# Linear attention's feature passes: the squares of the projections move from VectorE to ScalarE

## The reference, cut to what matters

```python
def softmax_kernel_features(data, proj, is_query):
    d = data.shape[-1]                                   # 16
    data_normalizer = 1.0 / math.sqrt(math.sqrt(d))      # 0.5
    ratio = 1.0 / math.sqrt(proj.shape[0])
    data_dash = jnp.einsum('bhnd,md->bhnm', data_normalizer * data, proj)
    diag_data = jnp.sum(jnp.square(data), axis=-1, keepdims=True) * 0.5 * data_normalizer * data_normalizer
    stab = jnp.max(data_dash, axis=-1, keepdims=True) if is_query else jnp.max(data_dash)
    return ratio * (jnp.exp(data_dash - diag_data - stab) + EPS)
q1 = softmax_kernel_features(q, proj_mat, is_query=True)
k1 = softmax_kernel_features(k, proj_mat, is_query=False)
kv = jnp.einsum('bhnm,bhnd->bhmd', k1, v)
z = 1.0 / jnp.einsum('bhnm,bhm->bhn', q1, jnp.sum(k1, axis=2))
out = jnp.einsum('bhnm,bhmd->bhnd', q1, kv) * z[..., None]
```

## Time and profile before

| | us |
|---|---|
| median of three runs | 2383.1 |
| lowest and highest | 2375.92, 2383.48 |
| span of the profiled execution | 2403.1 |
| TensorE busy | 1879.3 (78%) |
| VectorE busy | 1495.5 (62%) |
| ScalarE busy | 1074.7 (45%) |
| GpSimd busy | 395.9 (16%) |

### The profile page before, as it was taken

The page is one execution under the profiler, slowest core; times in us unless marked ns, Lnnn a source line. Parts: engine busy times, 40 slices in busy tenths (PEclk is TensorE's granted clock), DMA queues, the critical chain, the costliest instruction groups (busy, mean ns, idle before and its releaser), DMA issues. The chain is left out here.

```text
span 2403.1 us, 30974 instructions
## 1 busy us (share of the span) xinstructions
PE 1879.3 (78%) x9780; PEld 1007.5 (42%) x9804; DVE 1495.5 (62%) x2518; ACT 1074.7 (45%) x1896; POOL 395.9 (16%) x595
## 2 busy tenths in 40 slices
PE   3868788858876453777668877998899984999994
PEld 2745655535333320000022234442133333888883
DVE  4558449966010687999878876999788883111114
ACT  1100222214110476999979964342477661222220
POOL 5000000000112010222100003331033343222221
PEclk8989999968887575555589978997799996999997
DMA  3011110005797004443011008777666703566664
GB/s 85 1 39 31 48 31 27 20 10 229 309 411 314 20 0 127 127 127 123 18 32 40 26 16 119 130 132 107 83 88 95 97 28 135 195 201 203 202 203 184
DMA packets 147792, 264.98 MB, mean 110 GB/s; under 512 B 28864, under 2 KB 115985, under 8 KB 142678
## 3 DMA queue, kind: packets, MB, share of 16 engines
q1 hardware_dynamic: 135750, 242.10, 38.0%
q0 software_dynamic: 10768, 18.19, 2.3%
q10 hardware_dynamic: 1152, 3.15, 0.3%
HBM read 221.85 MB, written 57.71 MB: 116 GB/s over the span
## 5 line engine op out<-in xcount | busy, mean ns | idle before, releaser
L1743 PE MATMUL ps<-arena 128*128 x376 | 194.9, 621 | 108.2 <-ACT ps L1785 60.1
L1785 ACT ACTIVATE ps<-ps,arena 128x512 f32<-128x512 f32 x384 | 256.7, 1121 | 6.3 <-POOL arena L1769 6.3
L1753 DVE TENSOR_REDUCE arena<-ps 128x1024 f32 x192 | 232.8, 1225 | 24.5 <-PE ps L1743 12.2
L1785 ACT ACTIVATION_READ_ACCUMULATOR ps<-ps,arena 128x1 f32 x384 | 234.7, 668 | 0.0
L2159 DVE TENSOR_REDUCE arena<-ps 128x1024 f32 x192 | 221.3, 1219 | 12.4 <-PE ps L2405 9.8
L2618 ACT ACTIVATE arena<-ps 128x1024 f32<-128x1024 f32 x192 | 185.1, 1020 | 97.6 <-PE ps L2500 96.4
L2962 DVE TENSOR_TENSOR arena<-ps,arena 128x384 f32<-128x384 f32 x39 | 21.8, 558 | 286.4 <-PE ps L2918 286.4
L2942 ACT ACTIVATE arena<-ps,arena 128x256 f32<-128x256 f32 x234 | 89.5, 481 | 235.9 <-PE ps L2907 230.0
L2405 PE MATMUL ps<-arena 96*128 96x512 bf16 x500 | 162.7, 430 | 26.4 <-DVE arena L2159 12.2
L1950 ACT ACTIVATE arena<-ps 128x1024 f32<-128x1024 f32 x192 | 178.7, 1048 | 7.8 <-DVE arena L1970 4.6
L529 PE MATMUL ps<-arena 96*128 96x456 f32 (+1 forms) x512 | 170.3, 482 | 8.8 <-DMA arena<-la_xt 5.2
(11 more groups left out here) (394 smaller groups left out, 3264.8 us busy)
## 6 DMA issues: line engine op xcount, KB each, us to landing
arena<-in_sm_w_dram SPq DMA_DIRECT2D x128, 576.0 KB, 15.5
arena<-in_re_w_dram SPq DMA_DIRECT2D x39, 1252.0 KB, 5.9
arena<-ra_parts SPq DMA_DIRECT2D x192, 192.0 KB, 9.1
routed_in<-routed_in SPq DMA_DIRECT2D x8, 3332.0 KB, 14.2
ra_parts<-arena SPq DMA_DIRECT2D x48, 192.0 KB, 2.4
arena<-routed_in SPq DMA_DIRECT2D x39, 196.0 KB, 5.4
arena<-la_xt SPq DMA_DIRECT2D x16, 384.0 KB, 3.4
arena<-arena SPq DMA_DIRECT2D x64, 96.0 KB, 2.2
```

The costliest lines, as they stand in the source:

```text
L1743: ins = pe.matmul(ps[:, 2 * (n % 4) + t % 2, :], QM[j][:, h, t * P:(t + 1) * P], KI[:, b, h // HG, :], start=True, stop=True)
L1753: v.tensor_reduce(MXq[:, b, 2 * u:2 * u + 2, at_head(h)], ps[:, 2 * (n % 4):2 * (n % 4) + 2, :], AX.X, ALU.max).then_inc(s_lk, 1)
L1785: ins = act.activation(bank, bank, ACT.Exp, bias=nb[n % 4][:, t % 2:t % 2 + 1], scale=c_reg, accum_out=RS[:, b, t, at_head(h):at_head(h) + 1])
```

## The change

ScalarE computes the squares straight from PSUM with one activation per tile, in both passes, and VectorE's copy and multiply go. The signals `ks` and `qs` say that the squares are there; VectorE's chain waits for them and no longer for the products. In the key pass ScalarE's program becomes squares 0 and 1, the copy of the next batch's turned rows, squares 2 and 3. In the query pass it becomes, for t from 0 to 4: square t+1 (for t = 4 that of tile 0 of the next batch; none for t = 3), Exp t, copy of turn t-1. The row maximum moves ahead of the sum of squares in both passes, in the query pass with a semaphore of its own (`s_mq`).

```diff
+    def squares(act, b, t, ready, done):
+        ready.wait(act, b, t + 1)
+        act.activation(SQ[t % 2], ps[:, 2 * (t % 2), 0:D], ACT.Square).then_inc(done.sem, 1)
     def squared_lengths(v, link, t):
-        q = ps[:, 2 * (t % 2), 0:D]
-        link(v.tensor_copy(SQ[t % 2], q))
-        link(v.tensor_tensor(SQ[t % 2], SQ[t % 2], q, ALU.mult))
         link(v.tensor_reduce(dg[t % 2], SQ[t % 2].rearrange("p (h d) -> p h d", h=NH), AX.X, ALU.add))
...
+    ks = S1("k_squares", T, 1)
...
                 for t in range(T):
-                    kp.wait(v, b, t + 1)
+                    ks.wait(v, b, t + 1)
+                    v.tensor_reduce(MX[:, bass.ds(b, 1), t], features(t), AX.XYZ, ALU.max)
                     squared_lengths(v, link, t)
-                    v.tensor_reduce(MX[:, bass.ds(b, 1), t], features(t), AX.XYZ, ALU.max)
...
+            def square(b, t):
+                kd.wait(act, b, t - 1)
+                squares(act, b, t, kp, ks)
+            def batch(b, i, j, ahead):
+                square(b, 0)
+                square(b, 1)
+                if ahead:
+                    turned(b + 1, i + j, 1 - j)
+                square(b, 2)
+                square(b, 3)
...
             def chain(b, link, t):
                 j = t % 2
-                qp.wait(v, b, t + 1)
-                q = ps[:, 2 * j, 0:D]
-                v.tensor_copy(SQ[j], q)
-                link(v.tensor_reduce(mq[j].rearrange("p (g h) -> p g h", g=2), features(t), AX.X, ALU.max))
-                link(v.tensor_tensor(SQ[j], SQ[j], q, ALU.mult))
-                link(v.tensor_reduce(dg[j], SQ[j].rearrange("p (h d) -> p h d", h=NH), AX.X, ALU.add))
+                qs.wait(v, b, t + 1)
+                v.tensor_reduce(mq[j].rearrange("p (g h) -> p g h", g=2), features(t), AX.X, ALU.max).then_inc(s_mq, 1)
+                squared_lengths(v, link, t)
+                v.wait_ge(s_mq, b * T + (t + 1))
                 link(v.scalar_tensor_tensor(out=dg[j], in0=dg[j], scalar=0.125, in1=mq[j], op0=ALU.mult,
                                             op1=ALU.add))
...
+            def batch(b, i, j, ahead):
+                prev(act, num, i, j)
+                for t in range(T + 1):
+                    if t + 1 < T:
+                        squares(act, b, t + 1, qp, qs)
+                    elif t == T and ahead:
+                        squares(act, b + 1, 0, qp, qs)
+                    if t < T:
+                        qd.wait(act, b, t + 1)
+                        act.activation(QD[t % 2], QD[t % 2], ACT.Exp).then_inc(qe.sem, 1)
+                    if t:
+                        qt.wait(act, b, t)
+                        act.activation(Q1T[j][:, :, (t - 1) * P:t * P].rearrange("p (g a) q -> p g a q", g=2),
+                                       ps[0:2 * NF, 4:6, 0:3 * P].rearrange("p g (a q) -> p g a q", a=3),
+                                       ACT.Identity, bias=little[0:2 * NF]).then_inc(qc.sem, 1)
```

More of the change, by code:

```diff
@@ L563, in batch @@
             def batch(b, ahead):
-                link = Link(v, s_lk, b * (3 * T))
+                link = Link(v, s_lk, b * T)
                 for t in range(T):
-                    kp.wait(v, b, t + 1)
+                    ks.wait(v, b, t + 1)
+                    v.tensor_reduce(MX[:, bass.ds(b, 1), t], features(t), AX.XYZ, ALU.max)
                     squared_lengths(v, link, t)
-                    v.tensor_reduce(MX[:, bass.ds(b, 1), t], features(t), AX.XYZ, ALU.max)
                     v.scalar_tensor_tensor(
@@ L592, in _, with turned @@
             xc.start(act)
+            ks.start(act)
             for j in range(2):
                 act.sem_inc(s_xs[j], 1)
-            with act.Fori(0, B // 2) as i:
-                for j in range(2):
[L597 to L601, removed]
+            def turned(b, i, j):
+                xt.wait(act, b, 1)
+                prev(act, kp, i, j)
+                act.wait_ge(s_xs[j], 16 * i + 1)
+                act.activation(XTs[j], ps[0:DC, 4:6, :], ACT.Copy).then_inc(xc.sem, 1)
+            def square(b, t):
[8 more added lines that the diff above has]
+                square(b, 3)
+            turned(0, 0, 0)
+            with act.Fori(0, B // 2 - 1) as i:
+                for j in range(2):
+                    batch(2 * i + j, i, j, True)
+            batch(B - 2, B // 2 - 1, 0, True)
+            batch(B - 1, B // 2 - 1, 1, False)
         @block.sync
@@ L771, in linear_attention @@
         S1("q_turned", T, 2), S1("q_turned_copied", T, 2)
+    qs = S1("q_squares", T, 1)
     num, ot, pr, hh = S1("read_out", 2, 3), S1("normalised", 2), S1("projected"), S1("stream_updated")
-    s_qk, s_rd = sem("la_q_chain"), sem("la_reciprocal")
+    s_qk, s_rd, s_mq = sem("la_q_chain"), sem("la_reciprocal"), sem("la_q_max")
     xq = [sem(f"la_q_rows{j}_loaded") for j in range(2)]
@@ L826, in batch @@
             def batch(b, behind, last_behind):
-                link = Link(v, s_qk, b * (4 * T))
+                link = Link(v, s_qk, b * (2 * T))
                 chain(b, link, 0)
@@ L849, in _ @@
         def _(act):
-            for s in (qe, qc):
+            for s in (qe, qc, qs):
                 s.start(act)
-            with act.Fori(0, B // 2) as i:
-                for j in range(2):
[L854 to L864, removed]
+            def batch(b, i, j, ahead):
[13 more added lines that the diff above has]
+                                       ACT.Identity, bias=little[0:2 * NF]).then_inc(qc.sem, 1)
+            squares(act, 0, 0, qp, qs)
+            with act.Fori(0, B // 2 - 1) as i:
+                for j in range(2):
+                    batch(2 * i + j, i, j, True)
+            batch(B - 2, B // 2 - 1, 0, True)
+            batch(B - 1, B // 2 - 1, 1, False)
         @block.tensor
```

## The result

| | us |
|---|---|
| changed kernel, median of 20 runs | 2389.41 |
| before, median of 20 runs | 2378.06 |
| ratio, 95% interval | 1.0044 [1.0032, 1.0057] |
| span of the profiled execution, changed (before) | 2387.4 (2403.1) |

A forecast was written before the change was run, and what follows sets the result against it. Key pass bound by the latency of VectorE's chain, query pass by VectorE, then by a loop through all engines. Key pass -4.2 plus query pass +5.6 gave +1.4 us on 2383.1: 2384.5 us, eight-in-ten range 2373 to 2394.

The forecast's parts named there:

- likeliest case: Whole kernel: no change that runs can tell, +1.4 us to 2384.5 us, own range 2379 to 2391, chance 0.64.
- The square costs 0.35 us, seen as late as by VectorE: ScalarE, both passes: a square takes 0.33 to 0.36 us and starts after TensorE with VectorE's delay, about 0.1 us.
- The rival with a late square: ScalarE sees each product tile late; at 0.2 us more per square the total is +8 us, 2391 us; chance 0.14.
- Key pass -4.2: Key pass: shorter stops before the turn and at the batch end cut a batch from 12.72 to 12.2 us, eight times.
- Query batch 21.9, stop 1.93 released by the copy: Query pass: TensorE waits 1.93 us before turn 1 for ScalarE's copy behind square 2; batch 21.9 us against 21.52.
- The stepping: Query pass: following the three engine queues through a batch in order gave a batch of 21.9 us.
- The first rival: Query pass runs at TensorE's floor, batch about 20.2 us, because the copy isn't late: 2370 us; chance 0.13.
- Query pass +5.6: Query pass: 3.5 us longer in the first two batches, 0.4 in each of five more, tail the same within 0.2.
- The rival with the clock: Query pass: TensorE's clock falls to 1.2 GHz for half a batch in batch 0, 10 us: 2394 us; chance 0.06.
- Stages behind do not change: Stages before and behind the two passes, including the key-value pass, keep their times.

The follow-up runs named there:

- best: swap kernel with VectorE normalising the key pass's next batch of rows ahead of tile 0's chain: 2350.57 us, 0.9895 of before.
- swap: Changed kernel with ScalarE's square 2 in each query batch put behind Exp 1 and copy 0: ratio to before 0.9932, query pass 190.8 us.
- fill7: Changed kernel plus 7 small TensorE matmuls per query batch between product tile 2 and turn 1: ratio to before 1.0013, query pass 208.8 us.
- k_only: Changed kernel with the query pass put back to before's text, so only the key pass is changed: ratio to before 0.9977.
- wide: Changed kernel with ScalarE squaring 456 columns, not 192, in the query pass: ratio to before 1.0056, query pass 218.0 us.
- before_early: Kernel before with only one edit, key-pass rows normalised ahead of tile 0's chain: ratio to before 0.9957, key pass 100.6 us.
- q_only: Changed kernel with the key pass put back to before's text, so only the query pass is changed: ratio to before 1.0060.
- fill: Changed kernel plus 12 small TensorE matmuls per query batch between product tile 2 and turn 1: ratio to before 1.0038, query pass 212.8 us.

## Why the prediction was right or wrong

The forecast was no change at 2384.5 us, in a range that holds 2389.41; the kernel is slower by 0.32 to 0.57%, past the 0.3% line, so the likeliest case as I put it did not hold. That the range holds it is in part luck. It was set around the 2383.1 of three runs, and the median of 20 is 2378.06. As a change, the forecast was +1.4 us and the range ended at +10.9; the measured change is +10.5, between 7.6 and 13.6.

*The square costs 0.35 us, seen as late as by VectorE.* 0.330 measured for all 64; tile 2 starts at 408.43 and its square at 411.05, 2.62 as taken. The rival with a late square falls. The two forms in the Trainium skill (ScalarE: Activation LUTs, section "What ACT_TABLE_LOAD costs") come to 346 and 439 ns for 192 columns, an estimate by that page; the trace speaks for the first, which is 16 ns too high here.

*Key pass -4.2.* It was -5.1, batch 12.12 for 12.2: the stop before the turn is 1.14 us where I had 1.2, and the maximum starts 0.14 after the square. The mechanism (VectorE matters by latency only) holds, and the edit of best shows the rest of it.

*Query batch 21.9, stop 1.93 released by the copy.* 21.79 and 1.83. The stepping was right to 0.1 us, and swap shows that the order of ScalarE's queue is the cause. The first rival, a pass at TensorE's floor, did not come about in the changed kernel; swap's batch of 19.79 us is what it describes.

*Query pass +5.6.* It was +12.3. The step that failed is the one that kept TensorE's clock at 1.00: I compared the stop of 1.93 us with stops of 1.34 in the key pass, and gave the rival 0.06 and a place in batch 0 only. The dips came behind the stop in five of eight batches; batch 2 became 4.1 us longer by it, batches 5 and 6 1.7 each. With the clock held up in the steady batches (fill7) the pass takes 208.8, 5.7 above before. Of this, 3.2 us lie ahead of the first reciprocal (3.5 forecast for the first two batches), 1.8 in the next six batches (2.0 forecast), and 0.7 in the last (0.2 forecast at most). So the term was right with the clock at 1.00, and the other 6.6 us are the clock's. The rival with the clock (0.06, 2394) had the right mechanism and about the right size in the wrong place. The trace of before had a warning that I left out of the argument, TensorE at the end of its query pass:

```profile
494.07 0.83 PE L875 MATMUL ps<-arena 128*88 128x128 f32 x6 [1.12 <-ACT arena L862]
496.76 0.83 PE L875 MATMUL ps<-arena 128*88 128x128 f32 x6 [1.86 <-ACT arena L862]
499.18 1.01 PE L898 MATMUL ps<-arena 128*128 128x192 f32 x2 [1.59 <-DVE arena L814]
```

Behind waits of 1.12, 1.86 and 1.59 us the project takes 1.01 us, where it takes 0.59 in the steady batches.

*Stages behind do not change.* The key-value pass, whose code is untouched, took 71.9 us and not 69.8. TensorE was at the lower level for about 3.5 us longer there than before. The profiled kernels fall in the same groups: those with the longer stay (k_only, swap, fill7, wide, before_early) took 71.4 to 71.7 us, those without (q_only, best) 69.4 and 69.8, and fill, with a longer one still, 72.9. In all ten profiles the time of the pass goes with the length of that stay, so the clock very likely carries the 2 us; no run changed it alone, and why it comes back later in some stays open.

## What to carry to other kernels

When work moves to an idle engine, ask not how much room the engine has but what stands behind the new instruction in its queue: ScalarE had 15.7 of 21.5 us free, and a square that waits for the newest product held back a copy that TensorE needed for the next turn. Put an instruction that waits for the newest input behind those whose input is older. Idle time of TensorE is not all alike: look at its longest piece in a row, and at the durations of the matmuls behind it.

## What the runs showed of the hardware

Behind a single stop of 1.83 us, in batches in which TensorE is busy for 19.35 of 21.79 us, the granted clock fell to 1.2 GHz over the next tile in five of eight batches of the changed kernel and of q_only, and in the others it didn't. Behind stops of 2.05 us (wide) it fell in six batches in a row. Behind stops of 1.0 to 1.4 us (both passes before) it fell in no steady batch. With small matmuls in the stop, which write 32 partitions (fill7), it stayed at 1.00 through the steady batches.
